# Second scan layer: one more weight bank at the logarithms, and VectorE's product with C in odd states

## The reference, cut to what matters

```
dA = dlt[..., None] * A_log[None, :, :, None, :]
phi = jnp.exp(-jnp.cumsum(dA, axis=3))
dbx = dlt[..., None] * jnp.swapaxes(b, 2, 3)[:, :, None] * xs[..., None]
h = phi * jnp.cumsum(dbx / (phi + 1e-12), axis=3)
y = jnp.einsum('bkdln,bknl->bkdl', h, c) + Ds[None, :, :, None]
```

## Time and profile before

| | us |
|---|---|
| median of 3 runs (lowest, highest) | 15300.93 (15300.76, 15302.67) |
| the profiled execution | 15302.04 |
| its span, first to last instruction | 15299.9 |
| VectorE busy in it | 14142.6 |
| GpSimd, ScalarE, TensorE busy | 12419.2, 11996.8, 13023.2 |
| the scans of this layer | about 9838 to 12216 and 12640 to 15004 |

### The profile page before, as it was taken

The page is one execution under the profiler, slowest core; times in us unless marked ns, Lnnn a source line. Parts: engine busy times, 40 slices in busy tenths (PEclk is TensorE's granted clock), DMA queues, the critical chain, the costliest instruction groups (busy, mean ns, idle before and its releaser), DMA issues. The chain is left out here.

```text
span 15299.9 us, 186073 instructions
## 1 busy us (share of the span) xinstructions
PE 13023.2 (85%) x37976; PEld 5684.4 (37%) x37976; DVE 14142.6 (92%) x19364; ACT 11996.8 (78%) x26319; POOL 12419.2 (81%) x6712
## 2 busy tenths in 40 slices
PE   9999799999999889999999979877777677777776
PEld 3333244444444334444444435433333233333333
DVE  7778699999999989999999988899999979999998
ACT  6777678788888767878888855699889858988996
POOL 1111599999999879999999972599999859999996
PEclk9999899999999999999999989999999889999988
DMA  2110244444444334444444432233333213332331
GB/s 39 30 26 17 69 121 121 122 121 120 119 120 120 107 108 122 120 122 120 120 120 120 120 105 66 61 90 89 89 88 89 83 46 89 89 89 87 89 88 45
DMA packets 543491, 1416.85 MB, mean 93 GB/s; under 512 B 134802, under 2 KB 191274, under 8 KB 538778
## 3 DMA queue, kind: packets, MB, share of 16 engines
q1 hardware_dynamic: 542342, 1404.94, 32.5%
HBM read 1323.37 MB, written 58.28 MB: 90 GB/s over the span
## 5 line engine op out<-in xcount | busy, mean ns | idle before, releaser
L1205 PE MATMUL PS<-Hc,ident 128*128 128x448 f32 x16128 | 7100.2, 580 | 1452.2 <-POOL Hc L1595 1389.6
L1579 POOL TENSOR_TENSOR Tr<-du,BC 128x1344 f32<-128x1344 f32 x2684 | 6886.8, 2566 | 0.0
L1205 PEld LDWEIGHTS PS<-Hc,ident 128*128 128x128 f32 x16128 | 3091.0, 200 | 5346.3 <-issue 2793.0
L1595 POOL TENSOR_TENSOR Hc<-Hr,BC 128x896 f32<-128x896 f32 (+2 forms) x2688 | 4409.1, 1640 | 199.4 <-DVE Hr L1478 193.3
L1319 ACT ACTIVATE PS<-dl,A 128x448 f32<-128x448 f32 x5376 | 3402.4, 633 | 1009.5 <-DVE Hr L1478 689.3
L1478 DVE TENSOR_TENSOR_SCAN Hr<-PS,Tr 128x449 f32<-128x449 f32 x2688 | 2895.4, 1077 | 4.1 <-ACT PS L1319 3.4
L1478 DVE TENSOR_TENSOR_SCAN PS<-PS,Tr 128x449 f32<-128x449 f32 x2688 | 2837.1, 1077 | 60.8 <-ACT PS L1319 57.9
L1478 DVE TENSOR_TENSOR_SCAN Hr<-Ar,PS 128x449 f32<-128x449 f32 x2240 | 2417.2, 1079 | 0.0
L1329 ACT ACTIVATE PS<-cs,lneps,A 128x448 f32<-128x448 f32 x2688 | 1928.5, 719 | 138.2 <-DVE Hr L1478 75.0
L1485 DVE TENSOR_TENSOR Hc<-PS,BC 128x448 f32<-128x448 f32 x3136 | 1823.5, 605 | 0.0
L1454 DVE SCALAR_TENSOR_TENSOR PS<-PS,Tr 128x448 f32<-128x448 f32 x2688 | 1651.7, 614 | 154.9 <-ACT PS L1329 146.3
(11 more groups left out here) (288 smaller groups left out, 15088.0 us busy)
## 6 DMA issues: line engine op xcount, KB each, us to landing
BC<-bcscratch SPq DMA_DIRECT2D x5376, 224.0 KB, 3.6
zscratch<-zst SPq DMA_DIRECT2D x84, 224.0 KB, 1.9
bcscratch<-rows SPq DMA_DIRECT2D x336, 56.0 KB, 1.7
z<-zscratch SPq DMA_DIRECT2D x28, 672.0 KB, 4.9
rb<-rows SPq DMA_DIRECT2D x12, 1176.0 KB, 7.1
xg<-mid SPq DMA_DIRECT2D x12, 1176.0 KB, 8.1
xr<-mid SPq DMA_DIRECT2D x56, 168.0 KB, 2.7
rl<-rows SPq DMA_DIRECT2D x56, 168.0 KB, 3.3
```

Source lines behind the costliest of these rows:

```text
L1205: e.matmul(PS[:, YB + c, 0:T], K["ident"][:], Hc[:, g % NHC, c, :], start=False, stop=(nn == 15)).then_inc(y_done, 1)
L1579: e.tensor_tensor(Tr[:, g % NTR] if ratio else Tr[:, g % NTR, :, 1:TW], du[:, q % 2], b, ALU.mult).then_inc(t_done, 1)
L1595: e.tensor_tensor(Hc[:, g % NHC, m:3], Hr[:, g % NH, m - FIRST_SB:3 - FIRST_SB, 1:TW], c_, ALU.mult).then_inc(hp_done, 1)
```

## The change

A second weight of each tile leaves the ring: u = 31 goes to bank HB, where VectorE's states lie, between the product of state 9 and the scan of state 11. For that VectorE's product with C moves to odd states (`on_dve` is g % 2, and the two counting functions follow), a one-column activation writes the zero that the scan wants in the bank's first column, and the loop runs two weights further ahead at u = 29 and 30 instead of one. The first layer's values are the same as before.

```
     def on_dve(g):
-        return (1 if ratio else 2) - g % 2
+        return g % 2 if ratio else 2 - g % 2
...
     def products_before(g):
-        return (0 if ratio else g) + (g + 1) // 2
+        return g // 2 if ratio else g + (g + 1) // 2
...
     def kept_before(g):
-        return g + (g + 1) // 2 if ratio else 2 * g
+        return g + g // 2 if ratio else 2 * g
...
-    SPARE = BURST + 1
+    SPARES = {BURST + 1: XB, BURST + 2: HB}
...
         def weight_bank(u):
             q, r = divmod(u, 48)
-            return XB if r == SPARE else (u - q - (r > SPARE)) % NW
+            return SPARES[r] if r in SPARES else (u - len(SPARES) * q - sum(r > i for i in SPARES)) % NW
...
-                n += back % 48 != SPARE
+                n += back % 48 not in SPARES
...
-                    e.wait_ge(s_done, 48 * (q - 1) + SPARE + 1)
+                    e.wait_ge(s_done, 48 * (q - 1) + BURST + 2)
...
-                if u % 48 == SPARE:
+                if weight_bank(u) == HB:
+                    e.wait_ge(st_done, kept_before(16 * q + 9) + 1)
+                    e.activation(PS[:, HB, 0:1], still[:, 0:1], ACT.Copy)
+                elif weight_bank(u) == XB:
...
-                ahead = u + 4 if ratio and s in (BURST, BURST + 1) and q + 1 < NQS else u + 3
+                ahead = u + 5 if ratio and s in (BURST, BURST + 1) and q + 1 < NQS else u + 3
...
                 if c < on_dve(g) and g:
                     e.wait_ge(h_done, products_before(g))
+                    if ratio and nn == 11:
+                        e.wait_ge(s_done, 48 * q + BURST + 3)
```

## The result

The changed kernel takes 15364.9 us (median of 5 runs, 15349.07 to 15375.31) against 15300.93 (5 runs, 15300.7 to 15314.36): 1.0041 times as long, 95% interval 1.003 to 1.0053. The prediction was 15306, in a range of 15262 to 15338, with 0.14 for slower by over 0.2%. It was wrong: slower by 64 us where no measurable change was forecast.

The account below looks back on a forecast made before the run. ScalarE bounds the stretch from |delta| to past the logarithms, VectorE the rest; 40 x 0.31 - 14 x 0.21 - 4.2 = +5.3 us on 15302.04, less 1.1 for the median, gives 15306 us, range 15262 to 15338.

Parts of the forecast that it names:

- The loop: A tile's length runs VectorE's scan 41, last delta, GpSimd's work, gather, TensorE, ScalarE's full stretch, weight 35, next scan 41.
- (d): GpSimd's products before the gather and TensorE's chain after it: equal count, same distance and length, so no cost.
- (a): Weight 33 made before the logarithms' table load: work moved, not removed; the 1.4 us stall shrinks to 0.2 at weight 35.
- (b): New small ScalarE work before the logarithms, a one-column zero and a wait: 0.22 us per tile, 12 us in all.
- (c): VectorE has two products instead of one from input multiply 35 to scan 41: 0.515 us more per tile.
- (e): In 14 of 54 tiles the wait for TensorE's late last-delta sum covers the second product: -0.21 us each.
- (f): At each pair's end, GpSimd's shorter last product and one early addition save 2.1 us per pair, 4.2 in all.
- Rival 2: TensorE's last sum is late in every tile, 0.51 us more in 40: up to 15337 us; chance 0.14 beyond 0.2%.
- Rival 1: The stall at the logarithms goes and stays gone, ScalarE having more slack: 15241 or 15220 us; chance 0.15.
- Rival 3: The bank comes too late for weight 31: each 0.1 us costs 5 us, 0.3 gives 15322; within the forecast's 0.71.
- The signs named for a right forecast: Input multiply 33 waits nothing, 34 about 0.5, 35 about 1.0; tile 84.3 us; idle before input multiply 130 to 160 us.

Follow-up runs that it names:

- e2_states: Changed kernel with VectorE's products in states 0, 2, 4, 6, 9, 11, 13, 15 instead of the odd ones, extra weight kept: 15277.21 us, ratio 0.9983.
- e8_state2: Changed kernel with VectorE's product of state 1 moved to state 2: 15345.52 us, ratio 1.0024.
- e9_state6: Changed kernel with VectorE's product of state 7 moved to state 6: 15330.97 us, ratio 1.0016.
- e5_te_delta3: Changed kernel with the third delta alone moved ahead of state 6's additions in TensorE's list: 15314.8 us, ratio 1.0007.
- e1_odd_only: Changed kernel with products in odd states but without the second weight outside the ring and the zero activation: 15357.8 us, ratio 1.0036.
- e7_weights: Changed kernel with ScalarE's weights behind the logarithms one or two steps sooner in its own list, nothing added or removed: 15316.75 us, ratio 1.0006.

## Why the prediction was wrong, point by point

- **The loop** (how a tile's length comes about) held. The distance from GpSimd's last `inputs` to the end of its gather is 30.37 for 30.38 and 31.75 for 31.75, and each delay in a segment came out as tile length. It was the sign that I had named for (d) being void, and it held while (d) failed.
- **Step (d) failed**, in its sentence that TensorE's chain starts at the gather and is as long as before. I counted GpSimd's products up to the gather (right) and TensorE's steps behind it (right), but took state 2's additions ahead of it as done, and state 6's ahead of the third delta. They are six passes behind GpSimd's product instead of four. With no two of them done early, TensorE stands idle for longer ahead of them (2.33 us for 1.48 in the tile shown) and in two tiles of three runs them at the low clock. From the end of the gather to |delta| 2 it is 0.94 longer in the first tiles (21.84 for 20.90) and 1.05 in the later ones (21.94 for 20.89); summed over the 54 tiles of both pairs, 43.3 of the 58 us. e2_states, e8_state2, e9_state6 and e5_te_delta3 show it, each at its place. So the term that (d) put at nothing is the granted clock of the passes ahead of these two steps. At the upper level in both places the way to |delta| 2 would be 0.05 + 5.78 + 6.70 + 8.06 = 20.59, 0.3 shorter than before (e5_te_delta3, free of the second delay, has 20.65 in its later tiles): an estimate from these segments is that the low clock costs 43.3 + 54 x 0.3 = 60 us, of which the otherwise shorter way gives 16 back. Why the segments to |delta| 0 and |delta| 1 are 0.3 and 0.2 shorter stays open.
- **(a) and (b)**: i(33) and i(34) came as worked out, the table load's shift nearly (0.80 where I had 0.67). New small work is 0.30 per tile (0.25 less the 0.05 slot, and 0.10) where I took 0.22. I had not seen a 0.22 us wait of scan 33: in ScalarE's list the start values of the next state stand behind d(34). It falls into a stretch that waits for w(35) anyway.
- **(c)**: from the table load to the last delta I expected +0.515 for the second product, less what comes before. e1_odd_only has just this against the kernel before: 24.94 for 24.47 in tiles without a late sum, +0.47. Near, 0.05 short.
- (a) to (c) together were +0.31 per tile; measured, the two segments to the table load and on to the last delta give 0.80 - 0.38 = +0.42 in the later tiles. The mechanism was right, the size 0.1 short.
- **(e)**: right. In a tile with a late sum the two segments to the last delta were 7.61 + 25.07 = 32.68 and are 8.41 + 24.08 = 32.49: -0.19 where I had -0.21. (The trace has 15 such tiles of the 54, not 14.)
- **(f)**: at the end of the first pair VectorE goes on 8.1 us after its last scan's start (12227.38 to 12235.46); before it was 8.7 (12204.18 to 12212.84). So 0.6 (and 0.8 in the second pair), where I had 2.1. Here too the clock stands in the way, behind 3.55 us of idle time:

```profile
12226.61 7.63 PE L1205 MATMUL PS<-Hc,ident 128*128 128x448 f32 x12 [3.55 <-POOL Hc L1600]
```

The granted clock over these twelve passes is 0.62. In e7_weights the last four take 1.77 us, their short length, and VectorE goes on 5.9 us after its last scan's start (12211.49 to 12217.38), 2.8 less than before.

- **The rivals**: none of them was it. Rival 2 had the engine right and the place wrong, and neither it nor any other named the clock: the sum for the last delta was late in none of the 54 tiles. Rival 1 was refuted by the rows of i(34) and i(35), which wait 1.13 us together where i(33) and i(34) waited 1.25; its assumption that ScalarE had slack comes true only in another order of its list (e7_weights). Rival 3 didn't happen: ScalarE's read of state 9 waits for nothing.

So the parts that were worked out had the right signs, and the term that was put at nothing was about ten times their sum. The signs named for a right forecast failed with it: a tile of 85.0 us and not 84.3, and 196 us of waits before the input multiply and not 130 to 160.

## What to carry to other kernels

When a share of work moves from one step of a pattern to its neighbour, don't stop at equal sums: for every in-order engine, list what stands directly ahead of each step that another engine waits for, and ask for that item alone whether it got later or longer. Count TensorE's passes behind a wait at both clock levels: behind idle times of 2.1 to 4.1 us, six passes cost 3.5 to 4.9 us in two tiles of three here, and 2.5 in the rest. Ask whether a step still starts in time at the low level, and whether a change lengthens the idle time ahead of it. A weight that is made earlier is worth only what the last item of the same full stretch gains: here a changed order in ScalarE's list was worth 0.8 us per tile, the extra bank 0.3.

## What was not expected of the hardware

How much a short wait of TensorE can cost, and that it need not: behind 2.33 us the granted clock over six passes was 0.58, behind 3.28 us 0.50, behind 6.20 us 0.50 for 4.49 us; but behind 2.31 and 3.27 us it was 1.00 in other tiles of the same run. Behind the waits of 1.25 to 1.73 us shown here (the kernel before, e2_states, e9_state6) passes kept their short length, 1.77 for four; in one tile of the kernel before (10952.23) a wait of 1.94 us was followed by four in 2.73 us, at 0.62. No run here shows what decides between the two. Many of the later tiles of the changed kernel alternate: their third delta comes 8.87 or 10.34 after the second with the same instructions. A dependent small operation on ScalarE started 0.25 us after a 0.16 us one, 0.09 behind its end; without the wait it was 0.05 after its start.
